# A Mamba scan on four engines: every third product with C on GpSimd, and a new order for the spreads, copies and sums around it

## The reference, cut to what matters

```
A = -jnp.exp(A_log)

def step(h, inp):
    u_i, d_i, B_i, C_i = inp
    dA = jnp.exp(d_i[..., None] * A)
    h = dA * h + (d_i * u_i)[..., None] * B_i[:, None, :]
    y = jnp.einsum('bdn,bn->bd', h, C_i)
    return (h, y)
...
y_ssm = jnp.swapaxes(ys, 0, 1) + x_act * D_param
y = y_ssm * jax.nn.silu(z)
return y @ out_proj_w.T
```

## Time and profile before

| | us |
|---|---|
| median of 3 runs (1257.43 to 1260.14) | 1258.63 |
| the profiled execution, its whole time | 1258.89 |
| its span from first to last instruction | 1257.1 |
| VectorE busy over the span | 921.3 |
| GpSimd busy over the span | 599.4 |
| the stage of 64 steps, first scan to last product with C | 864.83 to 1103.67 |

### The profile page before, as it was taken

How to read it: one execution, slowest core, us unless ns; L and a number is a source line. 1 busy time by engine, 2 the same in 40 slices (tenths; PEclk the granted TensorE clock), 3 DMA queues, 4 the chain that set the end, 5 groups by cost and what they waited for, 6 DMA issues and landing times.

```text
span 1257.1 us, 12629 instructions
## 1 busy us (share of the span) xinstructions
PE 988.2 (79%) x3048; PEld 560.2 (45%) x3048; DVE 921.3 (73%) x1229; ACT 638.2 (51%) x1157; POOL 599.4 (48%) x432
## 2 busy tenths in 40 slices
PE   5849888388878984599999999876676776675896
PEld 2314343133326723488888888432222222224684
DVE  4684895999977568466666666587989998955564
ACT  4744657300054483255555555776555555453455
POOL 3010275566630033277777777303656565623572
PEclk9979899599998996699999999987989998997899
DMA  2000300000020000476666666000000000000661
GB/s 72 1 0 0 111 0 15 0 0 1 0 59 0 1 16 7 92 156 152 146 142 155 151 147 156 3 0 1 0 0 0 0 0 0 1 13 15 149 153 34
DMA packets 18639, 61.22 MB, mean 49 GB/s; under 512 B 2560, under 2 KB 12416, under 8 KB 12800
## 3 DMA queue, kind: packets, MB, share of 16 engines
q1 hardware_dynamic: 18608, 60.86, 20.7%
HBM read 59.15 MB, written 1.70 MB: 48 GB/s over the span
## 4 chain that ended last, share of the span: by engine, by line
PE 48%; DVE 34%; issue 6%; ACT 5%; POOL 4%; DMA 2%; DVEq 1%; SPq 0%; POOLq 0%; ACTq 0%
PE ps L351 46%; DVE g L1378 5%; DVE g L1177 4%; DVE tmp L1177 4%; DVE y L1628 3%; DVE g L1628 2%; ACT rstd L759 2%; ACT g L759 2%; DVE resid L1177 2%; DVE parts L1317 2%; DVE parts L1177 2%; POOL g L1164 2%; DVE g L1585 1%; POOL sq L1068 1%; DMA g<-coef_scratch 1%
## 5 line engine op out<-in xcount | busy, mean ns | idle before, releaser
L351 PE MATMUL ps<-parts 128*128 128x512 f32 x1800 | 449.8, 408 | 34.1 <-DVE g L1177 10.0
L351 PEld LDWEIGHTS ps<-parts 128*128 128x128 f32 x1800 | 345.1, 194 | 137.8 <-DVE parts L1177 17.9
L759 ACT ACTIVATE g<-ps 128x512 f32<-128x512 f32 (+4 forms) x310 | 183.0, 597 | 314.7 <-PE ps L351 285.1
L1107 POOL TENSOR_TENSOR parts<-g,parts 128x512 fp32r<-128x512 f32 x168 | 217.6, 1295 | 156.2 <-ACT parts L759 152.2
L1164 POOL TENSOR_TENSOR g<-g 128x1024 f32<-128x1024 f32 x64 | 150.3, 2353 | 137.9 <-ACT g L759 134.9
L351 PE MATMUL ps<-g,arena 128*128 128x512 f32 (+1 forms) x328 | 164.9, 645 | 62.0 <-POOL g L1151 23.5
L1177 DVE TENSOR_TENSOR ps<-g,ps 128x512 f32<-128x512 f32 x168 | 116.9, 696 | 112.6 <-PE ps L351 90.7
L759 ACT ACTIVATE parts<-g 128x512 fp32r<-128x512 f32 (+2 forms) x252 | 126.3, 534 | 30.9 <-DVE g L1177 15.8
L351 PEld LDWEIGHTS ps<-g,arena 128*128 128x128 f32 (+1 forms) x328 | 62.3, 201 | 162.9 <-issue 61.0
L1177 DVE TENSOR_TENSOR g<-ps,g 128x512 f32<-128x512 f32 x160 | 110.7, 692 | 32.7 <-DMA g<-coef_scratch 14.9
L1068 POOL TENSOR_TENSOR sq<-resid 128x512 f32<-128x512 f32 x32 | 35.9, 1122 | 198.5 <-DVE resid L1177 185.0
(11 more groups left out here) (172 smaller groups left out, 1067.7 us busy)
## 6 DMA issues: line engine op xcount, KB each, us to landing
g<-coef_scratch SPq DMA_DIRECT2D x80, 512.0 KB, 6.2
g<-in_moe_dram SPq DMA_DIRECT2D x42, 192.0 KB, 4.9
g<-in_rope_dram SPq DMA_DIRECT2D x1, 2048.0 KB, 8.5
arena<-in_weights_dram SPq DMA_DIRECT2D x1, 1348.5 KB, 5.8
arena<-in_weights_dram SPq DMA_DIRECT2D x1, 1028.5 KB, 4.8
g<-in_x_dram SPq DMA_DIRECT2D x4, 256.0 KB, 4.0
out_dram<-g SPq DMA_DIRECT2D x4, 256.0 KB, 2.5
arena<-in_weights_dram SPq DMA_DIRECT2D x1, 838.0 KB, 6.9
```

The costliest lines, as they stand in the source:

```text
L351: return nc.tensor.matmul(o, lhsT, rhs, start=start, stop=stop, **kw)
L759: return nc.scalar.activation(o, i, func, **kw)
L1107: pv.tensor_tensor(hid_lo[:, cols(c)], g[:, 6, (c % 2) * N:(c % 2 + 1) * N], hid_hi[:, cols(c)].bitcast(F32), ALU.subtract).then_inc(s["hl ...
```

## The change

Of the 64 steps, those with n = 1, 4, 7, 10, 13 (`BY_POOL`, 20 of 64) have their product with C made by GpSimd instead of VectorE. Since that needs C in SBUF, ScalarE copies it there first (`copy_c`, two places in `sq`). The products now have four homes instead of two (`tmp` and `rstd`), as have d*u*B (`g[:, 10]` and `g[:, 9]`, was two). TensorE spreads B four steps ahead, sums three steps behind. ScalarE makes a step's decays first, then saves the carry, then copies C where needed, then B for two steps on. The gate multiplication of a chunk reads the sum in PSUM directly (`sums_out` goes) and stands inside VectorE's list, three steps into the next chunk; the last one stands at the end. Hardware loops become straight code.

```diff
+STEPS = 16 * CHUNKS
+BY_POOL = [s for s in range(STEPS) if s % 16 % 3 == 1]
...
+
+        def two_halves(home, k):
+            return home[:, 2 * k * N:2 * (k + 1) * N].rearrange("p (i n) -> p i n", i=2)
+
+        def inflow(step):
+
+            return two_halves(g[:, 10 if step % 4 < 2 else 9, :], step % 2)
+
+        def with_c(step):
+
+            return two_halves(tmp if step % 4 < 2 else rstd, step % 2)
+
+        def c_copy(step):
+
+            k = BY_POOL.index(step) % 2
+            return sq[:, k * N:(k + 1) * N]
+
+        def by_pool(step):
+            return sum(k <= step for k in BY_POOL)
+
+        def by_dve(step):
+            return step + 1 - by_pool(step)
 
         block = ctx.enter_context(nc.Block())
...
@@ -679,58 +703,48 @@
...
-            def spread_b(n, c, step):
+                return sel_bc[:, n, :]
+
+            def spread_b(step):
 
                 at_least(pe, s["bs_ready"], step)
-                mm(ps[:, B_BANK, :], row(n), bc_rows[:, cols(c)]).then_inc(s["bb_bank"], 1)
-
-            def spread_c(n, c, step):
-                at_least(pe, s["hc_ready"], step)
-                mm(ps[:, C_BANK, :], row(n + 16), bc_rows[:, cols(c)]).then_inc(s["cb_bank"], 1)
-
-            def sum_n(nb, step, stop=False):
-                pe.wait_ge(s["hc_ready"], step + 1)
+                mm(ps[:, B_BANK, :], row(step % 16), bc_rows[:, cols(step // 16)]).then_inc(s["bb_bank"], 1)
+
+            def spread_c(step):
+                if step - 1 in BY_POOL:
+                    pe.wait_ge(s["c_copied"], by_pool(step - 1))
+                elif step:
+                    pe.wait_ge(s["hc_ready"], by_dve(step - 1))
+                mm(ps[:, C_BANK, :], row(step % 16 + 16), bc_rows[:, cols(step // 16)]).then_inc(s["cb_bank"], 1)
+
+            def sum_n(step):
+                if step % 16 == 0:
+                    c = step // 16
+                    at_least(pe, s["yg_ready"], c)
+                    for i in range(2):
+                        mm(ps[:, i, :], diag_d[:, i, :], G(i, c), True, False, skip_group_check=True)
+                if step in BY_POOL:
+                    pe.wait_ge(s["hc_pool"], by_pool(step))
+                else:
+                    pe.wait_ge(s["hc_ready"], by_dve(step))
                 for i in range(2):
-                    last = mm(ps[:, i, :], ident, tmp[:, (2 * nb + i) * N:(2 * nb + i + 1) * N], False, stop,
+                    last = mm(ps[:, i, :], ident, with_c(step)[:, i, :], False, step % 16 == 15,
                               skip_group_check=True)
                 last.then_inc(s["sum_done"], 1)
 
...
-                chunk_of_states(c)
-            chunk_of_states(CHUNKS - 1, True)
-            pe.wait_ge(s["yt_ready"], 2 * CHUNKS + 1)
+            spread_b(0)
+            spread_c(0)
+            for step in range(1, 4):
+                spread_b(step)
+            pe.wait_ge(s["mo_ready"], 1)
+            for step in range(STEPS + 3):
+                if step + 4 < STEPS:
+                    spread_b(step + 4)
+                if step >= 3:
+                    sum_n(step - 3)
+                if step + 1 < STEPS:
+                    spread_c(step + 1)
+            pe.wait_ge(s["yg_ready"], CHUNKS)
             for c in range(CHUNKS):
                 pe.wait_ge(s["yg_ready"], c + 1)
...
+            def copy_b(step):
                 act.wait_ge(s["bb_bank"], step + 1)
-                act.wait_ge(s["db_ready"], step + 1)
-                f(g[:, 8, k * N:(k + 1) * N], ps[:, B_BANK, :], ACT.Copy).then_inc(s["bs_ready"], 1)
-                hold(act, s["hs_done"], step + 1)
+                if step >= 4:
+                    act.wait_ge(s["db_ready"], step - 3)
+                f(g[:, 8, step % 4 * N:(step % 4 + 1) * N], ps[:, B_BANK, :], ACT.Copy).then_inc(s["bs_ready"], 1)
+
+            def state_step(step):
...
+                c, n = step // 16, step % 16
+                if step >= 2:
+                    act.wait_ge(s["hs_done"], step - 1)
                 for i in range(2):
-                    f(decays(nb, i), G(4 + i, c), ACT.Exp,
-                      scale=neg_a[:, bass.ds(n + 16 * i, 1)]).then_inc(s["da_ready"], 1)
-                if saved is not None:
-
-                    f(carried[:, :, bass.ds(saved, 1)], states((k + 2) % 4)[:, :, N - 1:N], ACT.Copy)\
-                        .then_inc(s["carry_saved"], 1)
-
...
+            def save_carry(step):
+
+                n = step % 16
+                act.wait_ge(s["hs_done"], step + 1)
+                f(carried[:, :, n:n + 1], states(step % 4)[:, :, N - 1:N], ACT.Copy).then_inc(s["carry_saved"], 1)
+
+            def copy_c(step):
+                act.wait_ge(s["cb_bank"], step + 1)
+                if by_pool(step) > 2:
+                    act.wait_ge(s["hc_pool"], by_pool(step) - 2)
+                f(c_copy(step), ps[:, C_BANK, :], ACT.Copy).then_inc(s["c_copied"], 1)
+
+            copy_b(0)
...
+            for step in range(STEPS):
+                state_step(step)
+                if step >= 2:
+                    save_carry(step - 2)
+                    if step - 2 in BY_POOL:
+                        copy_c(step - 2)
+                if step + 2 < STEPS:
+                    copy_b(step + 2)
             boundary(6)
...
+                    def b_times_du(step):
+                        pool.wait_ge(s["bs_ready"], step + 1)
+                        if step >= 4:
+                            pool.wait_ge(s["hs_done"], step - 3)
+                        pv.tensor_tensor(inflow(step), g[:, 6:8, cols(step // 16)],
+                                         g[:, 8:9, step % 4 * N:(step % 4 + 1) * N].to_broadcast([P, 2, N]),
+                                         ALU.mult).then_inc(s["db_ready"], 1)
+
+                    def states_times_c(step):
+                        pool.wait_ge(s["c_copied"], by_pool(step))
+                        pool.wait_ge(s["hs_done"], step + 1)
+                        if step >= 4:
+                            pool.wait_ge(s["sum_done"], step - 3)
+                        pv.tensor_tensor(with_c(step), states(step % 4),
+                                         c_copy(step).unsqueeze(1).to_broadcast([P, 2, N]),
+                                         ALU.mult).then_inc(s["hc_pool"], 1)
+
+                    for step in range(4):
+                        b_times_du(step)
+                    for step in range(STEPS):
+                        if step in BY_POOL:
+                            states_times_c(step)
+                        if step + 4 < STEPS:
+                            b_times_du(step + 4)
 
 
         @block.vector
...
+            def scan(step):
+
+                n = step % 16
                 dve.wait_ge(s["da_ready"], 2 * step + 2)
-                dve.wait_ge(s["db_ready"], step + 5)
-                hold(dve, s["carry_saved"], step + 1)
+                dve.wait_ge(s["db_ready"], step + 1)
+                if step >= 4:
+                    dve.wait_ge(s["carry_saved"], step - 3)
+                    if step - 4 in BY_POOL:
...
+            def times_c(step):
...
-
-
-            with dve.Fori(0, CHUNKS) as c:
-                scan(0, 0, 16 * c)
-                with dve.Fori(0, 3) as m:
...
+                    .then_inc(s["hc_ready"], 1)
+
+            def gate(c):
+
+                dve.wait_ge(s["sum_done"], 16 * c + 16)
+                tt(g[:, 2:4, cols(c)], ps[:, 0:2, :], g[:, 2:4, cols(c)]).then_inc(s["yg_ready"], 1)
+
+            scan(0)
+            for step in range(STEPS):
+                if step + 1 < STEPS:
+                    scan(step + 1)
+                if step % 16 == 3 and step > 3:
+                    gate(step // 16 - 1)
+                if step not in BY_POOL:
+                    times_c(step)
+            gate(CHUNKS - 1)
             boundary(6)
```

More of the change, by code:

```diff
@@ L274, in states, with decays @@
             return home[:, 2 * (k % 2) * N:2 * (k % 2 + 1) * N].rearrange("p (i n) -> p i n", i=2)
-        def decays(nb, i):
-            return ps[:, DA_BANKS[nb] + i, :]
+        def decays(step, i):
+            return ps[:, DA_BANKS[step % 2] + i, :]
+        def two_halves(home, k):
[11 more added lines that the diff above has]
+            return step + 1 - by_pool(step)
         block = ctx.enter_context(nc.Block())
@@ L697, in sum_n @@
                               skip_group_check=True)
                 last.then_inc(s["sum_done"], 1)
[L700 to L728, removed]
@@ L1028, in states_2_to_15 @@
-            def states_2_to_15(c):
-                for n in (2, 3):
-                    state_step(c, n, n, n - 2)
-                with act.Fori(1, 4) as m:
-                    for k in range(4):
-                        state_step(c, k, 4 * m + k, 4 * m + k - 2)
-            def sums_out(c):
-                hold(act, s["sum_done"], 16 * c + 18)
-                for i in range(2):
-                    f(G(i, c), ps[:, i, :], ACT.Copy).then_inc(s["yt_ready"], 1)
-            act.sem_inc(s["yt_ready"], 1)
```

(45 more changed lines are left out.)

41 lines of the change are left out of this document (3 added, 38 removed).

## The result

The changed kernel takes 1239.34 us in the median, the kernel before 1258.13 in the same comparison: ratio 0.984, 95% interval 0.982 to 0.986, so 18 to 22.5 us faster. The forecast was 1231.5 with a range of 1223 to 1244. The direction and that range hold, and so does the mechanism but for one step, the end of the stage; the gain is some 8 us smaller than forecast. All times here are medians of undisturbed executions; of the run with the sums one behind, one execution of four took 5288 us and is left out.

A forecast was written before the change was run, and what follows sets the result against it. VectorE was taken to set the pace inside a chunk. The terms -22.4 + 3.4 - 7.2 - 1.2 + 0.3 = -27.1 took 1258.9 to 1231.8, as a median 1231.5; range 1223 to 1244 for 8 in 10.

The forecast's parts named there:

- VectorE's work: In the 64 steps: 20 moved products at 1.12 us save 22.4, three gates add 3.4, leaving 205.4 us.
- GpSimd keeps up: In each chunk GpSimd's 21 products take 48.8 us against VectorE's 51.3; priced at nothing.
- the bound of 2.32 a product: GpSimd's products in a row inside a chunk: 2.32 us from start to start.
- the walk: After a moved step's scan: C copied at 2.4 us, GpSimd's products at 4.7 to 11.7, each some 4 us early.
- the late rival: GpSimd or C chain late: 0.5 us waiting per moved product adds 10 us, 1241; at 0.8, 1247; chance 0.20.
- Chunk ends: Stage idle falls from 14.4 to 7.2 us: 2.0 behind each of three gates, 1.2 at the stage's start.
- The start: Ahead of the 64 steps: first scan about 863.6 for 864.83, -1.2 us.
- The end: From last product to output product: 3.5 us for 3.25, from the sum, the gate and a release: +0.3.
- The same sum, 2.1: Behind the last product: the wait for the last sum stays 2.1 us, as before the change.
- The forecast's own range: Whole kernel, 1227 to 1236: gate stalls of 0.4 to 3.0 around 2.0, the start within 1; chance 0.50.
- The dearer scans: Rival in the stage: shared access makes 128 scans, 44 products, 3 gates dearer by 0.34 us each, 1292; chance 0.05.

The follow-up runs named there:

- seven a chunk: The combined kernel (sums one behind, D products at n = 8, ten extra B spreads) with seven products a chunk on GpSimd instead of five: 1236.52 us.
- the filled run: The changed kernel with ten extra spreads of B ahead of the B spread of n = 7 in chunks 1 to 3: 1230.01 us, ratio 0.977.
- the second trace of before: The kernel before, unchanged, run once more for its trace: 1257.73 us in its one execution.

## Why the prediction was right, and where it was off

**VectorE's work** (-22.4 + 3.4): right. Busy 204.2 for 205.4, and 22.2 us for the 20 products by the run without them.

**GpSimd keeps up:** right in what it costs, nothing: 2.353 us each, no scan waits for it, and the bound of 2.32 a product is borne out by seven a chunk within 1.4 us. But the walk that gave the products some 4 us of lead was too kind. Step 10 of the changed kernel, a moved one: its scans, the copy of C, GpSimd's product with C, the next three d*u*B, and the scans of step 14, which read the first of these:

```profile
896.47 2.45 DVE L1653 TENSOR_TENSOR_SCAN y<-ps,carry,g 128x512 f32<-128x512 f32 x2
...
900.51 0.60 ACT L773 ACTIVATE sq<-ps 128x512 f32<-128x512 f32 x1
...
903.04 2.36 POOL L1182 TENSOR_TENSOR rstd<-y,sq 128x1024 f32<-128x1024 f32 x1
...
905.35 7.00 POOL L1173 TENSOR_TENSOR g<-g 128x1024 f32<-128x1024 f32 x3
...
909.26 3.62 DVE L1653 TENSOR_TENSOR_SCAN y<-ps,carry,g 128x512 f32<-128x512 f32 x3
```

The copy is done 2.2 us behind the scans' end, as walked (2.4). But GpSimd begins the product with C at 4.1 and not at 2.4, because it still has d*u*B of earlier steps to make. The walk took it to be free. Its product for step 14 is ready at 907.7, 1.6 us early. From step 4 on the least lead is 1.4, near the 1.5 that the prediction gave for the start alone: where both engines' work is level, a backlog isn't worked off. The cover held, but with less to spare than the prediction set against the late rival. The prediction also gave the decays-first order no price at all. It is worth 12 us by the medians, 9.6 by the traced executions, of which 8.7 are idle time in the stage and 0.8 ahead of it.

**Chunk ends** (-7.2): mechanism right, size off. I took 2.0 for each gate, between 0.4 at full clock and 3.0 at the low one. The clock was low at all three, and they cost 2.90, 3.12 and 3.23; the filled run had the other end, 0.32. That is 3.2 us too little, only partly repaid at the start (0.80 for 1.2). The 14.4 us of idle that were to be saved were also on the high side: the second trace of before has 12.3. Nor were they all at the chunk ends: in the first trace 9.3 were there, 2.7 at the start of the stage and 0.58 ahead of each chunk's last product.

**The start** (-1.2): right. The idle ahead of the first scan is 2.56 for 3.87.

**The end** (+0.3): this step failed. "The same sum, 2.1" overlooked that the edit which puts sums three behind leaves four of them behind the last C spread, where there were two, and that spread waits for VectorE's product before last. VectorE's last gate waits 5.65 us for them and not 2.1, and the end is 3.7 longer; with sums one behind the wait is 2.21 and the end 3.5, as the prediction had it.

The sum with the measured terms, against the second trace of before: -19.9 VectorE's busy time (224.1 to 204.2), -1.8 idle in the stage (12.3 to 10.5), -1.3 the start, +3.7 the end, together -19.3, for 18.8 between the medians.

The range was met in part by luck. The forecast's own range, 1227 to 1236, missed; 1239.3 lies in the upper part that was added for a late GpSimd or C chain, and this rival did not occur (the C chain is late behind gates alone). What filled that part was the end, which was priced at 0.3, and the gates. The dearer scans did not occur either: 1.26 beside a GpSimd that is busy 192 of 215 us. The Trainium skill (SBUF — State Buffer, "SBUF: two separate sides") has the lock stand against a VectorE instruction with two SBUF inputs; the scans and products here have one of their two tensors in PSUM, and their times agree with it.

## What to carry to other kernels

When a piece is moved to a slower engine, count that engine's whole list against the bound's list in the same stretch, and stop one piece before they cross: here five of 16, with six worth nothing more. A lag put between a producer and an in-order consumer to hide latency comes back at the end of the loop (3.4 us here for two more sums), so take the shortest that hides it. Look at what a matrix engine's queue head waits for: here a pause of 2.9 us was paid a second time in clock, behind it. Work that is of no use but fills the pause gave 2.8 us back at each, and work taken out of the chain that follows the pause gave back part of it.

## What had not been expected of the hardware

Ten extra products of no use, some 2.2 us of TensorE's time at each of three gates, made the kernel 9 us faster, since the granted clock then stayed at 2.4 GHz in place of 1.2. The kernel before had the same low clock at its chunk ends, and its idle time in the stage differs between two executions by 2.1 us in all. Behind the same pause of 2.88 us for a gate the clock was back at 2.4 GHz between 2.9 us (B copied first, third gate) and 6.2 us (the same run, second gate) after the gate's end, so the idle time behind one gate of one trace is one sample.
